# First layer of a two-layer attention kernel, from the seventh batch on: the normalized x turned by block loads and VectorE instead of TensorE, and the second turning of y ahead of the values' product

## The reference, cut to what matters

```python
xn = layer_norm(x, norm_w, norm_b)
q = (xn @ q_w + q_b).reshape(Bx, Tx, H, -1)
k = (xn @ k_w + k_b).reshape(Bx, Tx, H, -1)
att = jnp.einsum('bnhl,bmhl->bnmh', q, k)
att = jax.nn.softmax(att + (1.0 - mask) * -1000000.0, axis=2)
v = ((xn @ v_w + v_b) * src_mask[:, :, None]).reshape(Bx, Tx, H, -1)
y = jnp.einsum('bnmh,bmhl->bnhl', att, v).reshape(Bx, Tx, Dx)
h = layer_norm(y, sb_norm_w, sb_norm_b) * (1.0 + scale) + shift
x = x + silu(h) @ out_w + out_b
```

## Time and profile before

| what | value |
|---|---|
| median of 3 runs | 890.01 us (888.34 to 890.52) |
| the profiled execution | 891.08 us, its span 889.1 us |
| busy share of the span | PE 96%, PEld 80%, DVE 88%, ACT 76%, POOL 69% |
| first layer in rounds | until about 485 us of the span |
| drain of the first layer, start of the second | about 485 to 560 us |
| granted TensorE clock, mean | 0.994 |

### The profile page before, as it was taken

The page is one execution under the profiler, slowest core; times in us unless marked ns, Lnnn a source line. Parts: engine busy times, 40 slices in busy tenths (PEclk is TensorE's granted clock), DMA queues, the critical chain, the costliest instruction groups (busy, mean ns, idle before and its releaser), DMA issues.

```text
span 889.1 us, 23631 instructions
## 1 busy us (share of the span) xinstructions
PE 856.3 (96%) x8304; PEld 707.8 (80%) x8304; DVE 780.8 (88%) x1609; ACT 671.3 (76%) x1200; POOL 615.6 (69%) x1095
## 2 busy tenths in 40 slices
PE   5899999999999999999999889999999999999996
PEld 4677777777777777777777558899999999999996
DVE  5789999999999999999998766899999998999976
ACT  2257777777677777777777884888888888888875
POOL 3456576666657575757565346898888888888875
PEclk9999999999999999999999989999999999999999
DMA  8853434344344434353434313222232323332101
GB/s 257 261 191 110 176 124 166 135 147 152 139 151 146 152 128 172 114 183 118 173 116 162 99 44 113 61 83 84 85 84 84 84 84 86 95 94 90 50 31 60
DMA packets 91237, 108.55 MB, mean 122 GB/s; under 512 B 8624, under 2 KB 61328, under 8 KB 90992
## 3 DMA queue, kind: packets, MB, share of 16 engines
q1 hardware_dynamic: 91120, 107.04, 36.7%
HBM read 35.60 MB, written 16.88 MB: 59 GB/s over the span
## 4 chain that ended last, share of the span: by engine, by line
PE 89%; DVE 3%; issue 3%; POOL 2%; ACT 1%; SPq 0%; DMA 0%; DVEq 0%; ACTq 0%; POOLq 0%
PE psX L1447 16%; PE psY L1568 13%; PE psT L1447 10%; PE psM L1447 10%; PE psT L1547 6%; PE psT L1526 5%; PE psY L1447 5%; PE psY L1593 3%; PE psM L1547 3%; PE psT L1458 3%; PE psT L1725 3%; PE psY L1678 3%; PE psM L1526 3%; PE psX L1605 2%; PE psM L1458 1%
## 5 line engine op out<-in xcount | busy, mean ns | idle before, releaser
L1037 DVE TENSOR_REDUCE sb_cm<-psT 128x4 f32<-128x1024 f32 x168 | 202.6, 1217 | 11.9 <-PE psT L1547 11.7
L618 ACT ACTIVATE sb_P<-psT 128x1024 f32<-128x1024 f32 x176 | 177.7, 1025 | 29.4 <-PE psT L1526 15.1
L1568 PE MATMUL psY<-sb_P,sb_Vp 128*17 128x256 f32 x2048 | 130.2, 383 | 1.8 <-DVE sb_yr L1063 1.2
L1037 DVE TENSOR_REDUCE sb_cm<-psM 128x4 f32<-128x1024 f32 x88 | 107.1, 1217 | 7.5 <-PE psM L1547 7.4
L418 POOL TENSOR_SCALAR sb_ve<-sb_mv 128x2 f32<-128x2 f32 x32 | 7.3, 229 | 125.0 <-DVE sb_mv L1071 124.9
L1447 PE MATMUL psX<-sb_xT,sb_W0h 128*128 128x256 f32 x488 | 93.6, 294 | 0.0
L618 ACT ACTIVATE sb_P<-psM 128x1024 f32<-128x1024 f32 x80 | 81.9, 1024 | 12.9 <-PE psM L1526 6.8
L1568 PEld LDWEIGHTS psY<-sb_P,sb_Vp 128*17 128x17 f32 x2048 | 50.3, 97 | 48.1 <-issue 5.4
L436 POOL TENSOR_TENSOR sb_qp<-sb_qp 128x512 fp32r<-128x512 f32 x64 | 82.1, 1283 | 5.3
L1547 PE MATMUL psT<-sb_Ks,sb_Qs 64*128 64x256 f32 x672 | 74.7, 304 | 2.7 <-DVE sb_cm L1037 1.4
L1526 PE MATMUL psT<-sb_Qs,sb_Ks 64*128 64x256 f32 x704 | 74.5, 296 | 2.4 <-ACT sb_P L618 2.2
(11 more groups left out here) (205 smaller groups left out, 2558.6 us busy)
## 6 DMA issues: line engine op xcount, KB each, us to landing
sb_Qs<-sb_qp SPq DMA_DIRECT2D x96, 256.0 KB
sb_Ks<-sb_qp SPq DMA_DIRECT2D x96, 256.0 KB
sb_xt<-in_x SPq DMA_DIRECT2D x32, 256.0 KB, 3.0
y_normed<-sb_Yn SPq DMA_DIRECT2D x32, 256.0 KB, 2.0
sb_u<-in_x SPq DMA_DIRECT2D x32, 256.0 KB, 3.0
sb_u<-y_normed SPq DMA_DIRECT2D x128, 64.0 KB, 2.5
out<-sb_v SPq DMA_DIRECT2D x31, 256.0 KB, 2.2
sb_v<-key_mask SPq DMA_DIRECT2D x32, 128.0 KB, 3.3
```

The lines of the kernel that those rows point to most:

```text
L618: a.activation(P[G % 4][:, :], pairs[place["S", n, g][0]][:, :], ACT.Exp).then_inc(s_ex, 1)
L1037: v.tensor_reduce(cm[n % 2][:, 4 * j:4 * j + 4], scores, AX.X, ALU.max, negate=True).then_inc(s_mx, 1)
L1568: ins = pe.matmul(psY[32 * j:32 * j + 17, y0:y0 + T], Vp[n % RING][:, m, 4 * gr + j, :], Pj[:, c0:c0 + 256], start=(m == 0), stop=(m == 1))
```

## The change

From batch 6 on (`BY_BLOCK = 6`), x takes the way that y already takes. POOL's `xnorm` writes into a tile xs in blocks, two batches ahead instead of one; SP stores it to a DRAM buffer `x_normed` (`nstore`) and loads it back with four DMAs (`nblocks`); DVE completes the turning with one 32x32 block transposition into xF (`xturn` on DVE); ACT's `xturned` reads xF; the subtraction `xlow` moves from DVE to POOL, where it is first in a round. PE's four transposing matmuls are gone in these rounds. `yturn(t-4, 1)` stands ahead of `vals(t)` on PE, and `divide(t-4, 1)` ahead of the new transposition and `vbias(t)` on DVE. DVE's statistics of x run two batches ahead; round 4 gets those of batch 6 on top. In the drain, three of DVE's four `yt_` stand earlier in its list.

The diff's core:

```diff
             for t in range(TURNS):
-                if ok(t + 2):
+                if ok(t + 2) and t < BY_BLOCK - 1:
                     sp.wait_ge(s_xn, t + 1)
                     xload(t + 2)
+                if ok(t + 3) and t >= BY_BLOCK - 1:
+                    sp.wait_ge(s_xn, t + 2)
+                    xload(t + 3)
                 if ok(t - 5):
                     ystore(t - 5)
+                if ok(t + 2) and t + 2 > BY_BLOCK:
+                    nstore(t + 2)
...
                 if ok(t):
                     parts(t, 1)
...
+                if ok(t + 2) and t + 2 >= BY_BLOCK:
+                    nblocks(t + 2)
...
+            def xlow(n):
+                g.wait_ge(s_xT, n + 1)
+                g.wait_ge(s_vm, n)
+                g.tensor_tensor(xT2[:, :, :].bitcast(F32R), xF[:, :, :], xT[:, :, :], ALU.subtract).then_inc(s_xl, 1)
...
             for t in range(B):
+                if t >= BY_BLOCK:
+                    xlow(t)
                 if ok(t - 5):
                     ynorm(t - 5)
...
+            def xturn(n):
+
+                v.wait_ge(s_nb, 64 * (n - BY_BLOCK + 1))
+                if n > BY_BLOCK:
+                    v.wait_ge(s_xl, n)
+                v.transpose(xF[:, :, :].rearrange("p i t -> p (i t)").rearrange("p (q b s) -> p b q s", q=4, b=4),
+                            xB[:, :, :].rearrange("p k t -> p (k t)").rearrange("p (b q c) -> p b q c", b=4, q=4))\
+                    .then_inc(s_xf, 1)
...
                 if t in RAMP:
                     xlow(t)
                 maxima(t, 1)
-                if ok(t) and t not in RAMP:
+                if t < BY_BLOCK and t not in RAMP:
                     xlow(t)
...
                 if ok(t - 4):
                     ystats(t - 4, 0)
+                if t >= BY_BLOCK:
+                    divide(t - 4, 1)
+                if t + 1 >= BY_BLOCK and ok(t + 1):
+                    xturn(t + 1)
                 if ok(t):
                     vbias(t)
-                if ok(t - 4):
+                if ok(t - 4) and t < BY_BLOCK:
                     divide(t - 4, 1)
+                if t + 2 == BY_BLOCK:
+                    stats(t + 2, 0)
+                    stats(t + 2, 1)
...
             yt_(0)
+            yt_(1)
             divide(B - 3, 0)
             v.wait_ge(s_sT, 8 * (B - 3))
-            yt_(1)
             h_(0, 0)
+            yt_(2)
             hl_(0)
             h_(1, 0)
+            yt_(3)
             x1_(0)
...
                 scores(t, 0)
-                if ok(t):
+                if t < BY_BLOCK:
                     xturn(t)
...
                 scores(t, 7)
-                if ok(t):
-                    vals(t)
-                if ok(t - 4):
+                if t >= BY_BLOCK:
+                    yturn(t - 4, 1)
+                vals(t)
+                if 4 <= t < BY_BLOCK:
                     yturn(t - 4, 1)
```

More of the change, by code:

```diff
@@ L42 @@
 RAMP = (2, 3)
+BY_BLOCK = 6
 def ok(n):
@@ L84, in bass_cond_seq_kernel @@
     nd = nc.dram_tensor("key_mask", (B, T), F32, kind="Internal").ap()
+    xnd = nc.dram_tensor("x_normed", (B, 128, 2 * D), F32, kind="Internal").ap()
     yd = nc.dram_tensor("y_normed", (B, 128, 2 * D), F32, kind="Internal").ap()
@@ L172, in bass_cond_seq_kernel @@
         yF = [sb(f"yF{i}", [128, 2, T]) for i in range(2)]
+        xs = sb("xs", [128, 4, 2, 2, 32])
+        xB, xF = (sb(n, [128, 2, T]) for n in ("xB", "xF"))
         W = [[w[:, n, :, :] for n in range(3)] + [Wo[l][:, :, :]] for l, w in enumerate((W0, W1))]
@@ L307, in parts, with nstore, nblocks @@
                 sp.dma_start(dst[1 + w:128:4, :, :], qp[w][:, 1, :, :]).then_inc(b, 16)
+            def nstore(n):
+                sp.wait_ge(s_xn, n + 1)
+                sp.dma_start(xnd[n], xs[:, :, :, :, :].rearrange("p a i k c -> p (a i k c)")).then_inc(s_nd, 16)
+            def nblocks(n):
+                sp.wait_ge(s_nd, 16 * (n - BY_BLOCK + 1))
+                if n > BY_BLOCK:
+                    sp.wait_ge(s_xf, n - BY_BLOCK)
+                by_block = xnd[n].rearrange("(b s) (a e) -> a s b e", s=32, a=4)
+                tile = xB[:, :, :].rearrange("p k t -> p (k t)").rearrange("p (b e) -> p b e", b=4)
+                for q in range(4):
+                    sp.dma_start(tile[32 * q:32 * q + 32, :, :], by_block[q]).then_inc(s_nb, 16)
             def c_in(n):
@@ L551, in _ @@
                     vmask(t - 1)
-                if ok(t + 1):
+                if t + 1 < BY_BLOCK:
                     xnorm(t + 1)
+                elif ok(t + 2):
+                    xnorm(t + 2)
                 if ok(t):
@@ L625, in xturned @@
             def xturned(n):
-                a.wait_ge(s_xtr, n + 1)
+                if n < BY_BLOCK:
+                    a.wait_ge(s_xtr, n + 1)
+                    src = psX[:, :].rearrange("p (k t) -> p k t", k=2)
+                else:
+                    a.wait_ge(s_xf, n - BY_BLOCK + 1)
+                    src = xF[:, :, :]
                 if n >= 1:
                     a.wait_ge(s_vm, n)
-                a.activation(xT[:, :, :].bitcast(F32R), psX[:, :].rearrange("p (k t) -> p k t", k=2),
-                             ACT.Identity).then_inc(s_xT, 1)
+                a.activation(xT[:, :, :].bitcast(F32R), src, ACT.Identity).then_inc(s_xT, 1)
             def qk(n, w):
@@ L675, in xn_ @@
                 else:
-                    a.wait_ge(s_xtr, B)
+                    a.wait_ge(s_xtr, BY_BLOCK)
                 for i in range(2):
@@ L1309, in _ @@
                 maxima(t, 2)
-                if t >= 1 and ok(t + 1):
+                if 1 <= t < BY_BLOCK - 1:
                     stats(t + 1, 0)
+                elif t >= BY_BLOCK - 1 and ok(t + 2):
+                    stats(t + 2, 0)
                 if ok(t - 5):
@@ L1360, in _ @@
             hl_(1)
-            yt_(2)
             ystats(B - 3, 0)
@@ L1373, in _ @@
             hl_(2)
-            yt_(3)
             divide(B - 1, 0)
@@ L1611, in qk @@
                     pe.wait_ge(s_xl, n + 1)
+                    if n >= BY_BLOCK:
+                        pe.wait_ge(s_vb, n)
                 elif n >= 2:
```

15 lines of the change are left out of this document (12 added, 3 removed).

## The result

The changed kernel takes 892.99 us, median of 20 runs (889.42 to 896.61), beside 888.58 us for the kernel before (886.05 to 892.12, 20 runs): 1.0045 times as long, 95% interval 1.0031 to 1.006. Two later groups of runs gave 1.0024 (1.0009 to 1.0039, and 1.0007 to 1.004). It is slower, by 2 to 4.5 us. The profiled execution of after took 891.38 us, its span 889.6 us at a mean granted clock of 0.998; that of before 891.08 and 889.1 us at 0.994. So the two profiled executions are nearly equal, and the loss has to be read in their parts.

The account below looks back on a forecast made before the run. PE bounds the old kernel; after the change DVE's loop through R2 does. Terms 3.4 + 0.8 - 0.2 - 0.6 give +3.4 us on 891.08, 894.5; against the median of 890.01, 893.4 us (+0.4%), range 884 to 898.

Parts of the forecast that it names:

- The turn: Between R1's and R2's reductions on DVE: nothing covers the wait for PE, 1.82 us start to start, 0.60 idle.
- PE has its time and can't use it: Steady rounds: PE loses 0.59 us of matmuls, could do 14.58 us, but waits for DVE ahead of R2.
- Rival A: Faster: PE stays the bound, rounds of 14.58 us, kernel 876, or 884 if DVE closes half; chance 0.13.
- The round: DVE's loop from one R2 reduction to the next: terms sum to 15.30 us, 0.13 above the old round.
- The estimate of 1.24 us: DVE's new 128x512 transposition by the skill's 311 ns per 128x128 square; set aside for 0.63 from a same-shape row.
- they and x's next load push back nothing that the round waits for: SP's queue: four block loads, 2.4 us of issue, and x's next load delay nothing needed; costed at nothing.
- Once only: Round 4's end: DVE's extra statistics of batch 6 take 1.1 us, partly absorbed by a 0.28 wait: +0.8.
- -0.2 for round 31: Round 31 has neither transposition nor subtraction, and its division no longer waits for v's product: -0.2 us.
- The drain: Last rounds: the second `yt_` leaves the chain, so one transposition of 0.63 us comes earlier: -0.6.
- rival C: No change: 0.6 us less wait keeps the drain's clock up at 515 to 520 us, 2.5 back, 891; chance 0.10.
- Rival B: Slower: POOL's subtraction exceeds its 0.6 us cover before q's product, 0.4 late per round, 904 us; chance 0.09.
- The rule that the prediction takes from the Trainium skill: DVE and POOL share a port pair; the second to come is blocked for a whole instruction, a possible cause of POOL's lateness.

Follow-up runs that it names:

- the experiment the other way round: The changed kernel with the last rounds' order as in the kernel before: 894.16 us, 1.0067 of before, 3.0 us above the changed kernel.

## Why the prediction was right, and where its sizes were off

The forecast was 893.4 us, +0.4%, by a bare turn at R2; 892.99 us were measured, and the turn is there. That the two times agree so closely is in part luck. The forecast started from 890.01 us for the kernel before, the median of three runs, and 20 runs have 888.58; the loss itself was forecast at 3.4 us and measured at 4.4, 2.5 and 2.1 in the three groups.

- **The turn.** Forecast: R1's reduction to R2's 1.82 us, with 0.60 idle. Measured 429.42 to 431.23, 1.81, with 0.60. It was taken from a single row of the drain. Two experiments show that it is the turn: 0.57 us of work moved into it from the rest of the round takes 0.60 us off the round, and 0.67 us of work added in it costs nothing.
- **PE has its time and can't use it.** Right: 0.45 us of wait ahead of R2, and four matmuls put back cost 1.3 us instead of 15. Rival A falls.
- **The round: 15.25 us, forecast 15.30.** The sum by its terms is R2 to the aggregation 10.40 (415.98 to 426.38; forecast 10.39), 0.10, division 0.61 (0.63), transposition 0.63 (0.63), v's bias 0.57 (0.60), R0 1.13, turn 1.81. The five hundredths matter: the loss is 0.08 us a round, 2.0 us in the 25 rounds of the table instead of 3.3. The transposition takes 0.63 us from start to start and 0.70 by itself. The estimate of 1.24 us, four times the figure in the Trainium skill (VectorE: DVE Perf Modes, The three transpose paths), isn't borne out for this shape; no run here has the 128x128 of 2 bytes for which the figure stands.
- **The step that failed: "they and x's next load push back nothing that the round waits for".** It looked at the steady rounds, where it holds. But with round 5 the statistics of x run two batches ahead instead of one, so that x of batch 7 is read in round 5, right behind R2, and no longer in round 6; its load stands behind the stores of q and k in SP's round 4. It costs some 2 us once, shown by moving it: 2.0 and 1.7 us in the traces, 2.1 by the medians with v's bias moved. In four of eight profiled executions a fall of the clock came behind it. A change of distance has to be walked through at its first round, load by load.
- **Once only: +0.8 forecast, +0.77 measured; -0.2 for round 31, -0.19 measured.**
- **The drain: -0.6 fits at equal clock, and the clock was left out of it.** At equal clock the order gains 0.3 to 1.3 us, by the medians 2.8, and 3.0 in the experiment the other way round. The difference goes with the clock, which the forecast left to rival C. Part of rival C may be in it. But in both orders the clock falls in some executions and less or not at all in others, so rival C's picture of a definite dip that a shorter wait removes isn't shown.
- **Rival B** falls: POOL's subtractions take 1.28 us each, mean of 26 1.277, as those beside them; its cover was enough. The rule that the prediction takes from the Trainium skill (SBUF — State Buffer, SBUF: two separate sides) holds there only against a VectorE instruction in a two-port mode or with two SBUF inputs. The subtraction at 413.99 runs beside reductions out of PSUM (413.04 to 415.38), so it doesn't test that rule.

The missed wait (+2.0 beyond the 0.1 forecast for that round) is more than the smaller loss in the rounds (-1.3) makes up for, and the larger gain of the drain takes off some more. The rounds and the wait together were forecast at 3.4 us and measured at 4.1. With the measured terms (+0.8 + 2.1 + 2.0 - 0.2, and -0.3 to -1.3 for the drain) the sum is +3.4 to +4.4 us, beside the 3.3 to 4.1 at equal clock.

## What to carry to other kernels

Two units that share a buffer and stand next to each other in both engines' lists make a turn: reader, writer, reader. Its 0.6 us are free only as long as some other instruction of the reader stands in it, so before an instruction is taken out of such a place, ask what takes its place; here an instruction of the same engine, free to move only because the change had taken x's turning out of the buffer that it reads, turned a loss of some 3 us into a gain of 12. And where a change makes a stage run further ahead, look at the first round of the new distance, where loads still come on the old one.

## What the runs showed of the hardware that I had not expected

- The turn from DVE over PE to DVE hardly varies where it is bare: the profile of the changed kernel has DVE idle for 0.60 us ahead of R2's reduction in each of rounds 6 to 31, and for 0.65 us in the drain. In a steady round it is 0.04 us from the end of R1's reduction to PE's start (415.39 to 415.43) and 0.55 us from there to DVE's start (415.98).
- Four transposing matmuls ahead of another group on PE cost 0.42 us a round and not the 0.58 that the chain gives them, since the group behind took 0.2 us less.
- The mean granted clock of an execution varies from 0.987 to 1.000 over the kernels here, and from 0.990 to 1.000 without any change of the program, and 0.006 of it goes with 3.8 us in the kernel before and 4.6 in the changed one. This is as large as the effect measured here, so the kernels were also compared at equal clock.
